# Attention scores in eight array tiles of 32 rows and 64 columns, with the front end in one PSUM bank and the value products one tile later

## The reference, cut to what matters

```
x = x + tanh(g_xattn[0]) * attention0(layernorm(x), ctx)          # 16 heads of 8
x = x + tanh(g_ffn[0])   * experts(layernorm(x))                  # 4 gated experts, hidden 256
x = x + tanh(g_xattn[1]) * attention1(layernorm(x), ctx, mask)    # the same with a 64 x 64 mask
x = x + tanh(g_ffn[1])   * ffn(layernorm(x))                      # quantised, depthwise convolution

attention: q = Wq xn + bq; k = Wk ctx + bk; v = Wv ctx + bv
           p = softmax(q k^T / sqrt(8)) per head; out = Wo (p v) + bo
```

## Time and profile before

| | before |
|---|---|
| median of 3 runs | 1122.85 us (1121.34 to 1123.03) |
| profiled execution, its own time | 1114.99 us |
| its span | 1113.2 us |
| PE busy | 1027.2 us (92%) |
| DVE busy | 855.4 us (77%) |
| ACT busy | 765.5 us (69%) |
| POOL busy | 664.6 us (60%) |

### The profile page before, as it was taken

The page is one execution under the profiler, slowest core; times in us unless marked ns, Lnnn a source line. Parts: engine busy times, 40 slices in busy tenths (PEclk is TensorE's granted clock), DMA queues, the critical chain, the costliest instruction groups (busy, mean ns, idle before and its releaser), DMA issues. The chain is left out here.

```text
span 1113.2 us, 34577 instructions
## 1 busy us (share of the span) xinstructions
PE 1027.2 (92%) x10842; PEld 768.2 (69%) x10842; DVE 855.4 (77%) x2430; ACT 765.5 (69%) x1666; POOL 664.6 (60%) x1367
## 2 busy tenths in 40 slices
PE   3899999999879899888888999999999879999996
PEld 2577777777668888887876666666666657777665
DVE  3677778777758888888866777777776759899986
ACT  2677777877566666666664777777777667777774
POOL 4856556574414555454787746464645248888883
PEclk9999999999879999999999999999999999999998
DMA  3410101100000000000000000000000000000000
GB/s 95 123 40 20 38 19 38 37 10 19 2 1 2 1 0 0 0 0 0 1 20 11 12 21 9 16 12 9 19 10 1 2 1 22 20 21 21 21 21 27
DMA packets 43756, 20.66 MB, mean 19 GB/s; under 512 B 7088, under 2 KB 43312, under 8 KB 43696
## 3 DMA queue, kind: packets, MB, share of 16 engines
q1 hardware_dynamic: 43696, 19.91, 6.4%
HBM read 15.70 MB, written 4.19 MB: 18 GB/s over the span
## 5 line engine op out<-in xcount | busy, mean ns | idle before, releaser
L797 DVE TENSOR_REDUCE smax<-score 128x16 f32<-128x1024 f32 x128 | 156.8, 1225 | 67.0 <-PE score L1115 55.6
L432 POOL TENSOR_SCALAR kj<-k_sb,const 128x512 f32<-128x512 f32 x256 | 173.2, 693 | 47.7 <-ACT k_sb L593 28.2
L805 DVE TENSOR_TENSOR prob<-score,smax 128x512 f32<-128x512 f32 x256 | 164.9, 686 | 1.2
L579 ACT ACTIVATE prob_t<-bank 128x512 f32<-128x512 f32 x256 | 139.4, 595 | 18.1 <-PE bank L1077 5.1
L1170 PE MATMUL bank<-vb,prob_t 128*64 128x18 f32 x4096 | 143.2, 213 | 6.3 <-ACT prob_t L579 5.4
L566 ACT ACTIVATE prob<-prob 128x512 f32<-128x512 f32 x256 | 147.5, 627 | 2.2 <-DVE prob L805 1.4
L1170 PEld LDWEIGHTS bank<-vb,prob_t 128*64 128x64 f32 x4096 | 130.6, 138 | 22.5 <-ACT prob_t L579 7.3
L1115 PE MATMUL score<-kj,q_sb 64*64 64x512 f32 x1024 | 140.3, 618 | 3.7 <-DVE prob L805 1.8
L1219 PE MATMUL bank<-ew,kj 128*128 128x128 f32 x1024 | 122.5, 278 | 19.7 <-DVE x_all L840 16.4
L1077 PE MATMUL bank<-const,prob 128*128 128x128 f32 x1024 | 135.9, 277 | 0.1
L1219 PEld LDWEIGHTS bank<-ew,kj 128*128 128x128 f32 x1024 | 116.7, 192 | 25.0 <-DVE x_all L840 19.2
(11 more groups left out here) (170 smaller groups left out, 2362.4 us busy)
## 6 DMA issues: line engine op xcount, KB each, us to landing
ctx_in<-in_ctx SPq DMA_DIRECT2D x32, 256.0 KB, 2.9
x_all<-in_x SPq DMA_DIRECT2D x32, 128.0 KB, 2.7
out_x<-x_all SPq DMA_DIRECT2D x128, 32.0 KB, 1.8
ew<-in_L_ffn_ew SPq DMA_DIRECT2D x2, 512.0 KB, 5.5
f_w<-in_L_ffn_w SPq DMA_DIRECT2D x2, 256.0 KB, 4.4
eb<-in_L_ffn_eb SPq DMA_DIRECT2D x1, 256.0 KB, 6.9
f_cb<-in_L_ffn_conv_b SPq DMA_DIRECT2D x1, 256.0 KB, 4.9
const<-in_const SPq DMA_DIRECT2D x1, 208.5 KB, 2.5
```

The source lines that it names most:

```text
L432: pool.tensor_scalar(kj[:, 1 - gpar, h, :], k_sb[:], const[:, C_J + h:C_J + h + 1], 0.0, ALU.mult, ALU.add).then_inc(s["kj_ready"], 1)
L579: act.activation(prob_t[:, 4 * half:4 * half + 4, :].rearrange("p i q -> p (i q)"), bank[2 + half], ACT.Copy).then_inc(s["p_copied"], 1)
L797: dve.tensor_reduce(smax[:], sc, AX.X, ALU.max).then_inc(s["smax_done"], 1)
L805: dve.tensor_tensor(prob[:, par, half * 512:(half + 1) * 512].rearrange("p (h k) -> p h k", k=S), sc[:, h, :], smax[:, h].unsqueeze(2).to_ ...
```

## The change

- Scores: q is cut in four blocks of 32 rows (4 heads each, JH = 4, RH = 4) instead of two of 64. `kj` has four copies instead of eight, and POOL makes four. Each of the eight products (4 blocks x 2 sequences) has 32 contraction rows, 64 output rows and 256 columns. The four blocks write the first 256 columns of banks 0 to 3, because banks 2 and 3 no longer hold transposed probabilities. DVE reads the scores through a four-dimensional view. In layer 1 there are four mask products of 256 columns for two of 512.
- Transposed probabilities: one bank (PT = 4) for both halves, and `prob_t` is double buffered. The second half's transposes wait until ACT has copied the first half.
- Front end: all pieces share one bank (FRONT = 5). Each piece is cut in two halves that stand at two places of the step, and their order is now transposes (j = 3), k (j = 0), q (j = 1), v (j = 2). Each piece waits until ACT has copied the one before it. At j = 3, ctx is the first half and x the second.
- Value products: those of tile t-2 in step t, in two halves of eight; everything behind them (`o_n`, its transpose, Wo, residual) moves one step later too, and each attention has one more step at its end.
- Experts: the hidden layer has a buffer of its own, and the gate product waits for `mx_hi_done` and `mx_lo_done`, since it shares the bank of the transposed x.

In the diff, which is cut, the line with `for h in` is POOL's, `copy_p` is ACT's, the `has(-3)` with `wait(dve` is DVE's, and the rest is PE's.

```diff
-JH, RH = 8, 2
+JH, RH = 4, 4
+SW = JH * S
+PT, FRONT = 4, 5
...
-        prob_t = sb("prob_t", [P, NPAIR, P])
+        prob_t = sb("prob_t", [P, 2, NPAIR, P])
...
-        hid = kj[:, 1, :, :]
+        hid = sb("hid", [P, EC, G * P])
...
-                        for h in ((), (0, 1), (2, 3, 4), (5, 6, 7))[j]:
+                        for h in ((), (0,), (1,), (2, 3))[j]:
...
+                    def copy_p(half):
+                        wait(act, "pv_mm", n - 2)
+                        wait(act, "p_tr", 2 * (n - 1) + half + 1)
+                        act.activation(prob_t[:, o, 4 * half:4 * half + 4, :].rearrange("p i q -> p (i q)"),
+                                       bank[PT], ACT.Copy).then_inc(s["p_copied"], 1)
...
-                    if has(-2):
-                        wait(dve, "pv_mm", n - 1)
+                    if has(-3):
+                        wait(dve, "pv_mm", n - 2)
...
                         for b in range(BT):
                             q = slice(b * S, (b + 1) * S)
                             g = slice(j * P + b * S, j * P + (b + 1) * S)
                             for r in range(RH):
-                                c = slice(r * 64, r * 64 + 64)
-                                last = pe.matmul(bank[r][q, :], q_sb[c, gpar, g], kj[c, gpar, :, g],
+                                c = slice(r * 32, r * 32 + 32)
+                                last = pe.matmul(bank[r][q, 0:SW], q_sb[c, gpar, g], kj[c, gpar, :, g],
                                                  start=(L == 0), stop=True, skip_group_check=True)
...
+                    def transpose_p(half):
+                        wait(pe, "exp_done", 2 * (n - 1) + half + 1)
+                        wait(pe, "p_copied", 2 * (n - 1) + half)
...
+                        if j == 0 and has(4):
+                            if half == 0:
+                                wait(pe, "xn_copied", n + 4 + G)
+                            last = pe.matmul(bank[FRONT][:, cols], w_t[:, L, 1, :], ctx_t[:, cols],
+                                             start=True, stop=True)
...
+                            if half == 0:
+                                pe.wait_ge(ctx_ld[gpar], group_loads(f, gpar))
+                                wait(pe, "v_ready", f)
+                            else:
+                                wait(pe, "a_xn_ready", f + G)
+                                wait(pe, "ctx_copied", f + G)
...
+                    front(0)
+                    if has(-3):
+                        wait(pe, "o_norm", n - 2)
+                        wait(pe, "x_attn", n - 3)
+                        tr(bank[7][:, 0:P], o_n[:, o, :]).then_inc(s["o_tr"], 1)
+                    if has(-1):
+                        transpose_p(0)
+                    front(1)
+                    if has(-2):
+                        values(0)
+                    if has(-1):
+                        transpose_p(1)
+                    if has(-3):
+                        wait(pe, "o_copied", n - 2)
+                        pe.matmul(bank[7][:, P:2 * P], o_t[:], w_t[:, L, 3, :], start=True, stop=True)\
+                            .then_inc(s["wo_mm"], 1)
+                    if has(-2):
+                        values(1).then_inc(s["pv_mm"], 1)
```

More of the change, by code:

```diff
@@ L596, in step @@
                         f = n + 3
+                        wait(act, "q_mm", f + G)
+                        wait(act, "scores_mm", f - G)
+                        act.activation(q_sb[:, 1 - gpar, :].rearrange("p (g b s) -> p g b s", g=G, b=BT),
+                                       bank[FRONT].rearrange("p (g s b) -> p g b s", g=G, b=BT),
+                                       ACT.Identity, bias=b_col[:, L, 0:1])\
+                            .then_inc(s["q_ready"], G)
+                    if j == 2 and has(2):
+                        f = n + 2
                         wait(act, "v_mm", f + G)
@@ new lines, in values @@
+                    def values(half):
+                        gp = gpar if j >= 2 else 1 - gpar
+                        v0 = (k - 2) % G * BT * NPAIR
+                        if half == 0:
+                            if j == 2:
+                                wait(pe, "v_ready", n - 2 + G)
+                            wait(pe, "o_norm", n - 2)
+                        wait(pe, "p_copied", 2 * (n - 2) + half + 1)
+                        for i in range(4 * half, 4 * half + 4):
+                            for b in range(BT):
+                                q = slice(b * S, (b + 1) * S)
+                                last = pe.matmul(bank[6][q, i * 2 * VW:(i + 1) * 2 * VW], prob_t[:, par, i, q],
+                                                 vb[:, gp, v0 + b * NPAIR + i, :, :].rearrange("p h v -> p (h v)"),
+                                                 start=True, stop=True, skip_group_check=True)
+                        return last
@@ new lines, in front @@
+                    def front(half):
+                        cols = slice(half * 256, half * 256 + 256)
+                        if j == 0 and has(4):
[3 more added lines that the diff above has]
+                                             start=True, stop=True)
+                            if half:
+                                last.then_inc(s["k_mm"], G)
+                        if j == 1 and has(3):
+                            if half == 0:
+                                wait(pe, "k_ready", n + 3 + G)
+                            last = pe.matmul(bank[FRONT][:, cols], w_t[:, L, 0, :], xn_t[:, cols],
+                                             start=True, stop=True)
+                            if half:
+                                last.then_inc(s["q_mm"], G)
+                        if j == 2 and has(2):
+                            if half == 0:
+                                wait(pe, "q_ready", n + 2 + G)
+                            for i in range(4 * half, 4 * half + 4):
+                                for h in range(2):
+                                    last = pe.matmul(bank[FRONT][h * S:(h + 1) * S, i * S:(i + 1) * S],
+                                                     ctx_t[:, i * S:(i + 1) * S], w_v[:, L, h, :],
+                                                     start=True, stop=True, skip_group_check=True)
+                            if half:
+                                last.then_inc(s["v_mm"], G)
+                        if j == 3 and has(5):
+                            f = n + 5
+                            if half == 0:
+                                pe.wait_ge(ctx_ld[gpar], group_loads(f, gpar))
[3 more added lines that the diff above has]
+                                wait(pe, "ctx_copied", f + G)
+                            for i in range(G):
+                                last = tr(bank[FRONT][:, i * P:(i + 1) * P], a_xn[:, i, :] if half else ctx_in[:, gpar, i, :])
+                            last.then_inc(s["xn_tr" if half else "ctx_tr"], G)
@@ L1142, in step @@
-                    if j == 0 and has(4):
-                        wait(pe, "ctx_copied", n + 4 + G)
-                        pe.matmul(bank[4], w_t[:, L, 1, :], ctx_t[:], start=True, stop=True).then_inc(s["k_mm"], G)
-                    if j == 1 and has(3):
-                        wait(pe, "xn_copied", n + 3 + G)
-                        for i in range(G * BT):
-                            for h in range(2):
-                                last = pe.matmul(bank[5][h * S:(h + 1) * S, i * S:(i + 1) * S],
-                                                 ctx_t[:, i * S:(i + 1) * S], w_v[:, L, h, :],
-                                                 start=True, stop=True, skip_group_check=True)
-                        last.then_inc(s["v_mm"], G)
@@ L1153, in step @@
-                    if j == 2 and has(2):
-                        wait(pe, "k_ready", n + 2 + G)
-                        pe.matmul(bank[4], w_t[:, L, 0, :], xn_t[:], start=True, stop=True).then_inc(s["q_mm"], G)
-                    if has(-2):
-                        wait(pe, "o_copied", n - 1)
+                        transpose_p(1)
+                    if has(-3):
+                        wait(pe, "o_copied", n - 2)
                         pe.matmul(bank[7][:, P:2 * P], o_t[:], w_t[:, L, 3, :], start=True, stop=True)\
```

182 lines of the change are left out of this document (72 added, 110 removed).

## The result

The changed kernel takes 1135.83 us (median of 4 runs, 1134.90 to 1136.24), the kernel before 1122.94 on the same chip. The ratio is 1.0109, with a 95% interval of 1.0084 to 1.0134: 1.1% slower. The forecast was 1119, slightly faster than before; its range of 1100 to 1138 held the measured time only through rival 2. The profiled execution took 1136.18 us with a span of 1134.3, beside 1113.2 before. Those 21.1 us are not the difference of the kernels. In these runs the time goes with the clock: 1117.97 us at 0.982, 1125.84 at 0.971. By the medians the kernels differ by 13 us.

What follows compares the result with a forecast made beforehand. PE was taken as the bound, DVE's loop two or three tenths of a microsecond behind. Steps -13.5 and -2.4 with edges +12.9 give -3 us; carried to the 1122.85 median, 1120, trimmed to 1119, range 1100 to 1138.

Steps and rivals of the forecast that it cites:

- rival 2: Every step: handing the bank between PE and ACT costs 0.2 to 0.3 us, leaving the edges' loss; 1136 us, chance 0.24.
- groups of both attentions: Four-tile groups, 15 per attention: 17.55 us falls to 17.1 and 18.84 to 18.3, saving 13.5 us.
- start of attention 0: One bank chains the pieces before the first scores, which start near 32.7 us instead of 29.01: +4 us.
- lead-in of attention 1, up to its first scores: Pieces ahead of attention 1's first tile: five copies come in between, two hidden or not waited for before; +3.9 us.
- end of attention 0: Gate product waits for a second copy and `mx_lo`, +1.3 us; the last tile's extra step and round, +2.2.
- end of attention 1: The last tile's longer round over PE, DVE and ACT, partly beside ffn work: +1.5 us.
- The scores: Score products on PE: eight tiles running together take 0.60 us for 1.02, giving 0.42 us a step.
- Cutting k and q in halves costs nothing that I can see: PE's k and q products: same columns, and weights load beside a 0.21 us stream, so no added cost.
- 0.42 - 0.19 = 0.23 us in three steps: PE alone, three steps of four: 0.42 gained on scores less 0.19 for two more changes of array form.
- ACT's wait once a group: Step behind the v copy: PE waits for ACT's ctx and probability copies, making it 0.5 us longer.
- DVE's loop: Value products through DVE's subtractions to scores: 8.22 us per two steps against PE's 8.12, stretching one step by 0.1.
- Rival 1: In the steps, ACT's wait doesn't come and DVE's loop alone sets them: groups 16.6 and 17.85, 1100 us, chance 0.26.

Runs made afterwards that it cites:

- the split: The kernel before, with its 16 value products cut in two halves around the output product Wo: 1155.72 us, ratio 1.0298.
- the first value products ahead: Changed kernel, in each fourth step the first half of the value products before the wait for ctx's copy, not behind x's transposes: 1134.52 us, 1.0117.
- the kernel before with filler: The kernel before, with 32 unread identity transposes at its two longest waits at the end of attention 0: 1118.43 us, ratio 0.9961.
- The combined kernel with all its filler: Changed kernel with value product halves joined, two banks in the lead-ins and 112 unread transposes at waits ending both attentions: 1095.41 us, ratio 0.9767.
- the combined kernel: Changed kernel with value product halves joined, two banks in the lead-ins and 56 unread transposes at the end of attention 0: 1102.82 us, ratio 0.9820.

## Why the prediction was wrong

The terms of the prediction's sum, beside the difference of the two traces (first and last scores, first hidden product and first ffn product on PE's timeline):

| | forecast, us | the two traces, us |
|---|---|---|
| groups of both attentions | -13.5 | -1.4 |
| last four steps of each | -2.4 | -3.1 |
| start of attention 0 | +4 | +4.2 |
| lead-in of attention 1, up to its first scores | +3.9 | +7.0 |
| end of attention 0 | +3.5 | +8.7 |
| end of attention 1 | +1.5 | +7.0 |
| ffn behind its first product | 0 | -1.4 |
| sum | -3 | +21 |

- **The scores** were right: 0.42 a step forecast, 0.40 measured, with the kernel that undoes them as the proof. (The terms of the 0.60 us add up to 0.58 or 0.64, by how the 0.03 is counted; 0.62 was measured.)
- **The step that failed first** is "Cutting k and q in halves costs nothing that I can see", and with it "0.42 - 0.19 = 0.23 us in three steps". The 0.19 for two more changes of form was right (0.21 measured in the split). But "the weights load beside a 0.21 us stream" fails where the form has just changed: there the load starts only with its product, and the first half of k pays 0.11 us. In the plain step the scores give 0.40. The value products in two halves take 0.11 back, and the rest 0.19: the change ahead of the first value products (0.10), the uncovered load of k's first record (0.11) and of the first transpose behind the value products (0.06), less the 0.07 that the transposes right behind the scores paid before. So 4.29 became 4.19 and not 4.06.
- **ACT's wait once a group** was right in its place and its first part (0.28 us for `ctx_t`, 0.3 forecast), and too small as a whole: 4.56 us forecast for the step, 4.72 and in every second group about 4.9 measured. So a group comes to 17.5 to 17.7 us and not to 17.1, and of the 13.5 us of the groups 1.4 are left (3.6 in the trace with the first value products ahead, where two early steps are about 1 us shorter each). Rival 2 came out with its number (1136), but by luck: in plain steps PE waits for nobody.
- **DVE's loop** is not seen: in the 480 us of the two long stretches the trace lists no wait of PE for DVE. Over the whole run its waits for the subtractions come to 2.7 us. In the plain last steps without front end, where the loop was expected, PE waits 0.26 us for ACT's first copy of the probabilities.
- **The start and the lead-in** were right in kind: 33.23 us for the forecast 32.7, the lead-in 11.8 for "near 11". What the sum lacked is the price behind the lead-in, where the hidden products ran at the lower clock: 7.0 us up to the first scores, not 3.9. (Up to 2.5 of this may be chance: the kernel before with filler, its code unchanged there, took 266.8 us for the 264.4.) With two banks the ratio falls from 1.0109 to 1.0016, 10.4 us for the forecast 8. That is nearly the whole slowdown.
- **The two ends** were forecast at 5 us and differ by 15.7 in the two traces. Two things are mixed in this. The first is the clock, which the prediction left out at the ends. At the end of attention 0 the changed kernel had 0.50, the kernel before 0.82. The combined kernel with all its filler had 1.00 there and took 21.02 us, not 26.45, and joining the value products alone did not shorten this stretch (26.99). That is 3.3 to 3.6 us over the two traces of the kernel before (17.77 at 0.82, and 17.46 at 0.90 with its filler), near the forecast 3.5; so there the missing term is the clock. At the end of attention 1 a part of the 7.0 is chance: the trace of the kernel before with filler, its code unchanged there, took 17.66 us at 0.76, where the profiled execution had 14.93 at 0.99. The changed kernel took 21.92 at 0.77, so 4.3 us are left for the forecast 1.5. The second thing, the longer round of the last tile, is the term that was too small there. These are comparisons of single traces. That the round costs what it does as a chain of dependent work is argued from the timelines and not shown: value products one tile earlier with all else unchanged was not tried.
- **Rival 1** counts the edges at 9 us where the forecast has 12.9, without a reason; with 12.9 its time would be about 1104 and not 1100. It didn't come in any case.

## What to carry to other kernels

Count the changes of the array's form in PE's order before splitting a run of equal tiles: here each cost 0.10 us, plus up to 0.11 where the next product's weights could not load ahead, and two of them with that ate three quarters of what eight tiles at once had given. Where pieces share one bank, look first at the stretches that have no other work to put between them: there two banks were worth 10 us. In the steady steps PE waited for a copy only where two pieces stood close together in the bank, 0.28 us once in four steps; two banks in the steps were not tried. A better order is found by what it leaves beside the waits of the other engines; the order with the fewest changes of form was no faster.

## What the runs showed of the hardware

- Sixteen records (eight fp32 products) of 32x64 tiles with 256 columns each, eight tiles at a time, take 0.62 us to the next work of another form. Their second round starts 0.22 us behind the first.
- Behind a change of form the weights of the next product are not loaded ahead: a load starts with its product (209.13 on the changed kernel) or, for the scores, 0.04 us ahead, and not the 0.11 us ahead that it is without a change (210.10 for 210.21), and k's first record takes 0.32 us for 0.21.
- The clock falls to its lower level at the ends of the attentions in both kernels and for a different length from run to run, 0.969 to 0.982 as a mean in the kernel before, and the time goes with it. With 56 idle transposes at the waits the combined kernel's runs had 0.975 to 0.978, with 112 of them 0.988 or 0.989 (0.986 to 0.993 with the gate computation moved).
